# Score operands staged in DRAM with the head dimension outermost, in a two-layer recurrent and attention kernel

## What is computed

```python
# B, T, D = 8, 512, 256; 16 heads of head dimension 16
xn = layernorm(x)
q, k, v = heads(xn @ Wq.T), heads(xn @ Wk.T), heads(xn @ Wv.T)     # each times 256 ** -0.5
scores = where(causal, q @ k.T * 16 ** -0.5, -inf)
s = merge_heads(softmax(scores) @ v) @ Wp.T * 256 ** -0.5
g = silu(experts(xn))                # top 2 of 32 low-rank experts for each token
x = x + s * g
```

## Time and profile before

| | us |
|---|---|
| Three runs | 1231.76, 2604.05, 1228.45; median 1231.76 |
| Profiled execution, device time | 1227.31 |
| Profiled execution, span | 1225.5, granted TensorE clock 0.936 |
| PE, PEld, DVE, ACT, POOL busy | 1069.8, 708.9, 510.6, 488.5, 256.6 |
| Operand transfers | 24 stores of 512 KB, 192 loads of 128 KB |

### The profile page before, as it was taken

One profiled execution on the slowest core, in us unless ns is written; L12 is line 12 of the kernel. 1 busy time (PEld: TensorE's weight loads), 2 busy tenths in 40 slices (PEclk: granted clock), 3 DMA queues, 4 the chain that ended last, 5 costly groups with the idle time before them and its releaser, 6 DMA issues.

```text
span 1225.5 us, 20586 instructions
## 1 busy us (share of the span) xinstructions
PE 1069.8 (87%) x6848; PEld 708.9 (58%) x6848; DVE 510.6 (42%) x1028; ACT 488.5 (40%) x1198; POOL 256.6 (21%) x237
## 2 busy tenths in 40 slices
PE   4699999999997557898799799889889889979986
PEld 2267777777775334555555565555555545546644
DVE  4611211212122233644744743653663564565461
ACT  2334444444444202263263264255246336326234
POOL 2200101101004223222321420521322322422000
PEclk8899999999998768899899999989989989989989
DMA  6530101011030075058039019119308506705700
GB/s 212 174 102 29 51 26 51 29 48 49 28 111 18 34 107 99 19 100 159 18 77 181 18 59 153 46 52 129 94 35 128 112 18 112 145 18 93 96 19 18
DMA packets 80501, 93.99 MB, mean 77 GB/s; under 512 B 9920, under 2 KB 72032, under 8 KB 80480
## 3 DMA queue, kind: packets, MB, share of 16 engines
q1 hardware_dynamic: 76256, 89.52, 35.1%
q10 hardware_dynamic: 4224, 4.19, 1.0%
HBM read 59.84 MB, written 33.59 MB: 76 GB/s over the span
## 4 chain that ended last, share of the span: by engine, by line
PE 70%; DVE 10%; issue 7%; ACT 5%; DMA 4%; SPq 2%; POOL 1%; DVEq 0%; ACTq 0%; POOLq 0%
PE PS L708 22%; PE PS L844 5%; PE PS L781 5%; PE PS L922 5%; PE PS L887 5%; DVE nm L1451 5%; PE PS L865 3%; PE PS L695 3%; PE PS L811 3%; PE PS L759 3%; DMA XT<-xt_d 2%; PE PS L948 2%; PE PS L790 2%; PE PS L889 2%; ACT arena L1184 2%
## 5 line engine op out<-in xcount | busy, mean ns | idle before, releaser
L708 PE MATMUL PS<-arena 128*128 128x256 f32 x1024 | 312.1, 421 | 0.0
L1451 DVE TENSOR_REDUCE nm<-PS 128x2 f32<-128x256 f32 (+3 forms) x256 | 200.9, 817 | 90.3 <-PE PS L867 89.3
L695 PEld LDWEIGHTS PS<-arena 128*72 128x72 f32 x1024 | 129.9, 141 | 68.1 <-ACT arena L1069 4.6
L1069 ACT ACTIVATE arena<-PS 64x8 f32<-64x8 f32 x512 | 88.5, 173 | 185.1 <-PE PS L695 181.4
L708 PEld LDWEIGHTS PS<-arena 128*128 128x128 f32 x1024 | 155.5, 192 | 0.0
L865 PE MATMUL PS<-K,Q 96*128 96x128 bf16 (+3 forms) x512 | 129.8, 319 | 25.0 <-DVE nm L1451 20.5
L1184 ACT ACTIVATE arena<-PS 128x1024 f32<-128x1024 f32 x128 | 128.5, 1029 | 29.2 <-PE PS L889 28.6
L887 PE MATMUL PS<-Q,K 98*128 98x512 bf16 (+3 forms) x512 | 122.8, 318 | 16.6 <-DVE nm L1451 14.1
L1311 DVE SCALAR_TENSOR_TENSOR arena<-arena 128x512 f32<-128x512 f32 x16 | 11.1, 694 | 267.7 <-ACT arena L1080 267.7
L695 PE MATMUL PS<-arena 128*72 128x8 f32 x1024 | 121.3, 191 | 0.0
L867 PE MATMUL PS<-negmask,identb 128*128 128x128 bf16 x512 | 105.6, 228 | 0.0
(11 more groups left out here) (161 smaller groups left out, 1399.9 us busy)
## 6 DMA issues: line engine op xcount, KB each, us to landing
qk_d<-QB SPq DMA_DIRECT2D x24, 512.0 KB, 2.9
Q<-qk_d SPq DMA_DIRECT2D x96, 128.0 KB, 8.9
K<-qk_d SPq DMA_DIRECT2D x96, 128.0 KB, 9.5
X<-in_L_attn_x SPq DMA_DIRECT2D x12, 512.0 KB, 13.5
arena<-xt_d SPq DMA_DIRECT2D x16, 256.0 KB, 3.2
gt_d<-arena SPq DMA_DIRECT2D x16, 256.0 KB, 2.5
wx_d<-arena SPq DMA_DIRECT2D x16, 256.0 KB, 2.0
XT<-xt_d SPq DMA_DIRECT2D x8, 512.0 KB, 9.9
```

Of the source, the lines that this page charges most:

```text
L695: pe.matmul(PS[0:WIDE, 7, 0:B], w_ab, HB[:, step], start=True, stop=True).then_inc(c_mm.sem, 1)
L708: mm = pe.matmul(o, lhs, rhs, start=first, stop=last)
L1451: v_.tensor_reduce(nm[:, i, 2 * hp:2 * hp + 2], PS[:, 2 * (u % 3):2 * (u % 3) + 2, 0:(i + 1) * P], AX.X, ALU.max, negate=True).then_inc(m_ ...
```

## The change

The DRAM tensor `qk_d` gets the shape (piece, query or key, feature in head, head, token) in place of (piece, query or key, feature, token). The pairs are put in an order in which equal query pieces follow each other, and the key pieces count up from 0 (`BLOCKS`). A half is loaded with six transfers: for each block of 3, 2 or 1 pairs, one for the query piece, read once for each pair, and one for the key pieces; a row of a transfer is 8 heads by 512 tokens, 8 KB. Each of the three stores becomes four, one for each 128 partitions of query or key, in rows of 1 KB as before. The semaphores' counts follow; nothing is computed in another way but for the order in which the six products lie in the contraction.

```diff
--- before.py
+++ after.py
@@ -23,7 +23,8 @@
 EPS = 1e-5
 SPLIT = 3
 
-PAIRS = [(0, 0), (0, 1), (1, 0), (0, 2), (2, 0), (1, 1)]
+PAIRS = [(0, 0), (0, 1), (0, 2), (1, 0), (1, 1), (2, 0)]
+BLOCKS = [(0, 3), (3, 2), (5, 1)]
 KS = len(PAIRS) * HD
 KM = KS + 2
 SCORE_SCALE = float(D) ** -1.0 * float(HD) ** -0.5
@@ -70,7 +71,7 @@
         gt_d = nc.dram_tensor("gt_d", (B, P, KT, T), F32, kind="Internal").ap()
         wx_d = nc.dram_tensor("wx_d", (B, P, NT, D), F32, kind="Internal").ap()
         x1_d = nc.dram_tensor("x1_d", (B, P, NT, D), F32, kind="Internal").ap()
-        qk_d = nc.dram_tensor("qk_d", (SPLIT, 2, D, T), BF16, kind="Internal").ap()
+        qk_d = nc.dram_tensor("qk_d", (SPLIT, 2, HD, H, T), BF16, kind="Internal").ap()
 
 
 
@@ -255,10 +256,10 @@
         q_s = count("q_s", 2 * SPLIT)
         q_d = count("q_d", 2)
         q_r = count("q_r", 2)
-        q_st = dcount("q_st", SPLIT)
+        q_st = dcount("q_st", 2 * KT * SPLIT)
         x_sv = dcount("x_sv", 1)
         x_ld = dcount("x_ld", 1)
-        q_ld = [dcount(f"q_ld{n}", 2 * len(PAIRS)) for n in range(2)]
+        q_ld = [dcount(f"q_ld{n}", 2 * len(BLOCKS)) for n in range(2)]
         v_mm = count("v_mm", 2)
         v_e = count("v_e", 2)
         v_c = count("v_c", 1)
@@ -424,23 +425,26 @@
 
                 for n, ready in enumerate((2, 5, 6)):
                     sp.wait_ge(q_s.sem, q_s.at(b, ready))
-                    sp.dma_start(qk_d[n].rearrange("c (m p) t -> p (c m) t", p=P), QB[:, n]
-                                 ).then_inc(q_st.sem, 16)
+                    for c in range(2):
+                        for m in range(KT):
+                            sp.dma_start(qk_d[n, c, :, m * H // 2:(m + 1) * H // 2].rearrange("d h t -> h d t"),
+                                         QB[:, n, c * KT + m]).then_inc(q_st.sem, 16)
 
             def load_operands(b, a, before=None):
 
-                sp.wait_ge(q_st.sem, q_st.at(b, SPLIT))
+                sp.wait_ge(q_st.sem, q_st.at(b, 2 * KT * SPLIT))
                 hold()
                 if before is not None:
                     sp.wait_ge(t_mm.sem, t_mm.at(before, (a + 1) * TU // 2))
                     hold()
-                rows_of = slice(a * D // 2, (a + 1) * D // 2)
                 heads = slice(a * H // 2, (a + 1) * H // 2)
-                for r, pair in enumerate(PAIRS):
-                    for c, dst in enumerate((Q6, K6)):
-                        sp.dma_start(dst[r * HD:(r + 1) * HD, heads, :],
-                                     qk_d[pair[c], c, rows_of].rearrange("(h d) t -> d h t", d=HD)
-                                     ).then_inc(q_ld[a].sem, 16)
+                for at, n in BLOCKS:
+                    first = PAIRS[at][0]
+                    rows_of = slice(at * HD, (at + n) * HD)
+                    sp.dma_start(Q6[rows_of, heads, :],
+                                 qk_d[first:first + 1, 0, :, heads].broadcast_to([n, HD, H // 2, T])
+                                 ).then_inc(q_ld[a].sem, 16)
+                    sp.dma_start(K6[rows_of, heads, :], qk_d[0:n, 1, :, heads]).then_inc(q_ld[a].sem, 16)
 
             def take_maxima(b, a):
                 sp.wait_ge(m_h.sem, m_h.at(b, a + 1))
@@ -968,7 +972,7 @@
                 for u in range(NT * H // 2):
                     if u % (NT * H // 4) == 0:
                         half = q_ld[u // (NT * H // 4)]
-                        pe.wait_ge(half.sem, half.at(b, 2 * len(PAIRS)))
+                        pe.wait_ge(half.sem, half.at(b, 2 * len(BLOCKS)))
                     scores(b, u)
                     run(side, u)
```

## The result

The changed kernel takes 1434.53 us in the median (1430.69 to 1436.45), the kernel before it 1230.11. The ratio is 1.1667, with a 95% interval of 1.1624 to 1.171; it leaves out the one run of the kernel before at 2604.05 us. The forecast was 1389, in a range from 1300 to 1470: the direction and the mechanism came true, the forecast fell 45.5 us short. The profiled execution has a span of 1434.1 us, 208.6 more than before.

A forecast was written before the change was run, and what follows sets the result against it. TensorE was taken to bound the kernel, with transfers nearly hidden. Late XT and slow clock added 128.9 us and interference 28.7 to 1227.3, making 1384.9; with the profiled execution 4.5 below the median, 1389, range 1300 to 1470.

The forecast's parts named there:

- What bounds it: Whole kernel: TensorE holds 70% of the chain of waits, DMA 4%, so a faster operand load has little to win.
- Engines by outermost index: Operand loads: a transfer is dealt out by its outermost index, so 3 or 2 pieces run on 3 or 2 engines.
- Rivals 1 and 2: Operand loads: all 16 engines move every load, 1216 (12%); or 16 engines still at 114 GB/s, 1232 to 1242 (5%).
- An engine's rate: Operand loads: one engine makes 25.8 GB/s, so a row of 8 KB takes 0.32 us.
- The queue sum: Steady batch, engine 0: store, half 0, S1, half 1 and XT take 47.4 us from half 0's first issue.
- the unknown interference: Operand loads: engines 0 and 2 writing partitions 0 to 15 and 32 to 47 together cost 0 to 8.2 us, taken 4.1.
- Rival 3: Operand loads: the engines hinder each other throughout, in half 1 too, 16.4 us for each of seven batches, 1476 us (8%).
- Half 0 and S1 just hidden: Steady batch: half 0 lands at 855.2, before unit 0 at 857.15, and S1 at 856.5, before `finish` at 858.15.
- The clock: Experts after the wait for XT: slow matmuls at 1.2 GHz cost 4.3 us a batch, already paid in the first batch.
- The sum: All batches: 128.9 us of later experts and last batch, plus 28.7 of interference, on 1227.3 give 1384.9.
- Stores: Stores ahead of half 0: outermost length 8 gives 8 engines, 3.0 us for 1.5, so half 0 starts 1.5 us later.

The follow-up runs named there:

- one pair per load: Changed kernel with twelve loads a half, one for each pair, the 16 features outermost, same layout, rows and stores: 1226.93 us, ratio 0.9981.
- the block of three at row 32: Changed kernel with the block of three pairs moved to rows 32 to 79 and that of two to 0 to 31: 1398.83 us, ratio 1.1402.

## Why the prediction was right, and where its size was off

*What bounds it.* Right. Transfers were nearly hidden, 8 KB rows alone bought nothing (one pair per load: 118 GB/s), and all the good that a faster load can do is 1%.

*Engines by outermost index.* Right, and shown: shares of 0.19 and 0.13, and 1434 against 1220 us for the exchange of two dimensions. The row that the forecast read it from was thin: the 0.1 us of the maxima's load hold five packets of 1 KB, too few to tell 3 engines from 8. The experiments carry the point, not that row. By the Trainium skill's rule (DMA: Bandwidth & Descriptors, section Why a DMA increments its semaphore by 16 and not by 1), an outermost 3 gives three engines, 16 sixteen; the trace agrees, 0.19 against 1.03. Rivals 1 and 2 are out.

*An engine's rate.* 25.8 GB/s was taken, 26.5 measured for two engines with the queue to themselves (53 GB/s).

*The queue sum.* This is where the size was off. From the first load to XT's landing the forecast had 45.9 us (47.4 less the store's 1.5) and 4.1 for the unknown interference, 50.0; it was 57.3. The unknown was 11.4 us, not 4.1, and beyond the upper end of 8.2 as well. It had two parts, and the bound saw one of them: engines 0 and 2 on rows that share. That part came out near the 4.1: the block of three at row 32 takes it away, and XT lands 3.9 us earlier. Some luck was in it, since no row had placed it between the two ends. The other part, about 7.5 us, was in no term: engines 0 and 1 slowed by whatever 14 others do meanwhile (one-pair loads, S1, and in the end XT's own batch). The forecast had halved the interval between two ends, and both ends left that part out.

*Where in the queue.* Half 0 was complete 31.6 us after the first load (817.23 to unit 0, which waited for it, at 848.86), where the sum without the store has 22.3 (1.0, 21.0 and 0.3): 9.3 more. From there to XT it was 25.7 in place of 23.6: 2.1 more. So nearly all of it fell in half 0. The forecast's guess that half 1 would be hindered less held.

*Rival 3.* The forecast named TensorE's waits at units 0 and 16 as the sign that the engines hinder each other throughout, and both waits came, the one at unit 16 in the last batch; half 0 was complete within 0.4 us of rival 3's time (31.6 against 32.0 after the first load). The sign misled: the sharing of rows accounts for 5.1 of the 9.3 us, 4.2 are left for the slowing by other engines, and half 1 did not repeat it. The time lies between forecast and rival, 45.5 us from 1389 and 41.5 from 1476.

*Half 0 and S1 just hidden.* Wrong, by the same term: unit 0 waited 7.63 us and `finish` 8.09. As the forecast said of this case, it mostly fell inside the wait for XT.

*The clock.* 4.3 us a batch forecast, 4.6 measured (17.8 less 13.2). That the first batch's loss was already paid came true too: its experts take 17.5 us in both kernels (498.43 to 515.93, and 472.30 to 489.76 before).

*The sum.* From the first load of the first batch to that of the last it is 882.3 us (441.83 to 1324.16), against 681.7 before (440.93 to 1122.65): 200.6 more, where the forecast had 128.4 and 28.7. The missing 43.5 are 6.2 a batch: XT 7.3 later than forecast, less the 1.5 of the stores, which did not show, and 0.3 for the clock. The last batch added 7.1 (109.9 from its first load to the end, against 102.8), where 0.5 was forecast: half 1 landed 53.8 us after the first load instead of 44.6, and unit 16 waited. The remaining 0.9 lies ahead of the first load.

*Stores.* 1.5 us was taken. One pair per load has the same stores, and its time is that of before within 0.4%, so in the steady batches they are hidden. In the changed kernel the first load follows the end of the stores' row by 2.8 us (814.46 to 817.23), before it by 2.9.

Open: why two engines lose rate while 14 others move data. The stretches show that they do (11 GB/s in place of 26.5), and the packets of 8 KB, up to 1.22 us in place of 0.31, show it too. The destination partitions are a likely place, since partitions that share are what slowed engines 0 and 2. But no run had the 14 engines write elsewhere, and nothing here rules out the DRAM side.

## What to carry to other kernels

Before a transfer is made larger, look at which index stands outermost on both sides: with 3 or 2 there, 3 or 2 engines did the work of 16 here, and what was issued later on the same queue waited for them. An exchange of two dimensions was worth 15% here, at the same number of transfers and bytes. Read the DMA share together with GB/s: a share of 0.19 with a queue that is never empty was a transfer on three engines, and the changed kernel's own trace showed it before any experiment. And where a load is late, first ask what stands ahead of it: moving one group of issues was worth as much as the better layout.

## What was not expected of the hardware

- An issuer can be held by two or three late engines. With engines 0 and 1 behind, single issues of operand loads on SyncE took 4 to 7 us, up to 13.5 (at 704.61), where they had taken 0.43, though a DMA share of 0.19 (827 to 846) left 13 of 16 engines idle.
- Rows of 8 KB and rows of 1 KB into 16 partitions ran at the same rate, 118 and 114 GB/s.
- Three engines at the same share made 59 GB/s on rows 0 to 47 and 79 on rows 32 to 79; a shift of rows was worth some 35 us.
- Two engines fell from 26.5 to about 11 GB/s each while 14 others were moving data.
